# A feed-forward's output product as three products of rounded halves, split by ScalarE and GpSimd

## The chip, the cores and the metric

The kernel runs on one core of a Trainium2 chip. It has five engines: TensorE (PE; its weight loads are shown apart, as PEld), VectorE (DVE), ScalarE (ACT), GpSimd (POOL) and SyncE (SP, here it only issues DMAs). The metric is the device time of one execution in microseconds (us). Lower is better.

## The reference

A decoder of two layers on x [16 sequences, 112 rows, 256 features] with a context of 375 rows. Each part adds to x what it computes from the normalised x. Only the last one is touched:

```python
logits = x @ Wg.T + bg                       # 4 experts, the two best of each row count
w = the softmax weights of the two best, else 0
base = x @ Wi.T                              # 1024 features
lora = (x @ A[e].T) @ B[e].T                 # rank 4, one for each expert e
h = relu(base + lora)                        # [row, expert, 1024]
out = sum_e w[e] * (h[e] @ Wo.T)             # Wo: 256 x 1024
x = x + out
```

All is float32.

## The kernel before

The program is a sequence of phases, each one block in which every engine has its own instruction stream, ordered by hand. Engines wait for each other by semaphores only. The last two phases matter here.

**Last phase (`l1_experts`, tiles named `l1f_`).** The 16 sequences are worked through in G = 4 groups of GB = 4, so a group has GT = 448 rows of x. The 1024 hidden features are FC = 8 chunks f of 128. For the two experts of a row the hidden values are `z_first` and `z_first + change`, and what the output product needs is `h = relu(z_first) + ratio * relu(z_first + change)`, a tile of 128 x 448 for each f.

TensorE, for a group (the body at L2568 to L2585): for each f one product for `change` (L2566), then the products of chunk f + 2 for `z_first`: two wide ones in float32 (L2524, each recorded as two instructions) and one narrow one (L2552). Chunks 0 and 1 of the next group come behind f = 7. Then the output product: for each sequence j of the group eight products, h[f, 112 rows of j] (weights, 112 columns) by wo[f] (moving, 256 columns), summed in one bank of `y_ps` (L2583). In the float32 form each is recorded as two instructions. For j = 0 it waits before each f for the h of that f, since VectorE may still be at work on it. Narrow products, L2552 and L2566, are of kind fp32r already: values that were rounded to fewer bits, for which the engine makes a single pass.

ScalarE copies `z_first` out of its bank (L2495). VectorE makes three instructions for each f: L2451 `z_second = z_first + change_ps` (one input in SBUF, one in PSUM), L2454 `z_second = max(z_second, 0) * ratio_rows` and L2459 `h = max(z_first, 0) + z_second` (both with two inputs in SBUF). Behind f = 7 it takes the four sequences' results out of `y_ps` (L2466), each when TensorE is done with it. GpSimd does nothing in these loops. Groups 1 and 2 run in a loop on the chip (`over_steps`), groups 0 and 3 are written out.

**The phase before (`l1_context_mix`, tiles named `l1x_`).** Its four groups end with a normalisation. VectorE works through, for a group, 4 x (L2165 sum, L2168 and L2170 statistics), 4 x L2174 (`z`, two inputs in SBUF), then waits for `y_rstd`, 4 x L2182 (new x, two inputs in SBUF), 4 x L2186 and L2190 (statistics of x). GpSimd, for a group: L2132 (`y_in` of the next group), 4 x L2149 (x plus a row vector), L2137 and L2139 (`y_rstd` from the statistics), L2125 and L2127 (`rstd` of the group before). SyncE loads the weights of the last phase during it, `l1f_wo` among them.

The same split into rounded halves is used in `l0_cross_attention` (tiles `l0x_`): L987 to L989 and L996 to L998 are three fp32r products each.

## Time and profile before

| | |
|---|---|
| median of 3 runs | 1867.79 us (1864.09 to 1875.49) |
| the profiled execution | 1861.0 us, its span 1859.2 us |
| mean granted TensorE clock | 0.965 of full |
| busy: PE | 1689.0 us, 91% |
| busy: VectorE, ScalarE, GpSimd | 1009.9, 740.9, 658.7 us |
| GpSimd in `l0_cross_attention`, slices 7 to 22 of the span | four to five tenths busy |

The span is that from the first to the last instruction. The last phase fills it from 1690.8 us on, its loops from 1739.6 us. A granted clock of 1.00 is 2.4 GHz, 0.50 is 1.2 GHz. A matmul's recorded duration contains its way through the array; what it costs in a row of matmuls is the distance of their starts. In the rows below "128*112 128x256" reads: weights of 128 rows and 112 columns, moving tile 128 x 256. Every view gives fp32r and float32 tiles as f32 where TensorE reads them.

### The profile page before, as it was taken

How to read it: one execution, taken by the hardware profiler on the slowest of the kernel's cores; microseconds unless marked ns; L12 is line 12 of the kernel's file. 1: busy time of each engine (PE TensorE's matmuls, PEld its weight loads, DVE VectorE, ACT ScalarE, POOL GpSimd, SP SyncE). 2: the span in 40 equal slices, each digit the busy share in tenths (PEclk: the TensorE clock that was granted, in tenths of full speed). 3: DMA queues.
4: the chain of work that ended last, by engine and by line, in shares of the span. 5: the costliest groups of instructions: out<-in, count | busy, mean ns of one | idle time of the engine just before them, and what ended most of it. 6: DMA issues, size and time to landing. Idle time of an engine off the chain costs nothing. (4 is left out here: it accounts for less than half of the span.)

```text
span 1859.2 us, 32555 instructions
## 1 busy us (share of the span) xinstructions
PE 1689.0 (91%) x11198; PEld 1331.6 (72%) x11198; DVE 1009.9 (54%) x2462; ACT 740.9 (40%) x2093; POOL 658.7 (35%) x559
## 2 busy tenths in 40 slices
PE   7899899999999999999999967999889688886898
PEld 6677677777777777777777756899688466554666
DVE  5466465665555665665555532232363577655664
ACT  2255344454444444454444412343113566541210
POOL 1022245555444555554454514343500233352000
PEclk9899999999999999999999979999989799997999
DMA  3100200000000000000000035753300000010000
GB/s 95 54 1 1 98 22 10 10 10 9 9 9 0 9 9 9 9 9 9 9 3 6 1 102 170 246 182 123 103 20 1 1 1 1 1 56 1 0 20 20
DMA packets 48803, 67.39 MB, mean 36 GB/s; under 512 B 11826, under 2 KB 42770, under 8 KB 46034
## 3 DMA queue, kind: packets, MB, share of 16 engines
q1 hardware_dynamic: 47186, 62.66, 10.8%
q0 software_dynamic: 1536, 3.67, 0.6%
q8 instruction: 48, 0.79, 0.2%
q14 instruction: 33, 0.27, 0.0%
HBM read 57.02 MB, written 9.31 MB: 36 GB/s over the span
## 5 line engine op out<-in xcount | busy, mean ns | idle before, releaser
L688 POOL TENSOR_SCALAR l0x_p<-l0x_p,l0x_inv 112x488 f32<-112x488 f32 x256 | 387.2, 1524 | 365.6 <-DVE l0x_inv L782 365.6
L891 ACT ACTIVATE l0x_p<-l0x_s,l0x_low 112x488 f32<-112x488 f32 x256 | 178.4, 697 | 288.0 <-DVE l0x_low L771 288.0
L771 DVE CUSTOM_DVE_ANT_0 l0x_s<-l0x_score_ps,l0x_bias 112x488 f32<-112x488 f32 x256 | 160.3, 664 | 128.5 <-PE l0x_score_ps L1031 117.2
L758 DVE TENSOR_TENSOR l0x_kT_lo<-l0x_proj_ps,l0x_kT_hi 128x488 fp32r<-128x488 f32 x128 | 85.3, 667 | 104.3 <-ACT l0x_kT_hi L881 104.3
L1039 PE MATMUL l0x_pT_ps<-ident,l0x_p 112*122 112x112 f32 x1024 | 124.8, 262 | 13.9 <-POOL l0x_p L688 13.8
L1039 PEld LDWEIGHTS l0x_pT_ps<-ident,l0x_p 112*122 112x122 f32 x1024 | 107.8, 139 | 35.4 <-POOL l0x_p L688 22.8
L1904 POOL TENSOR_TENSOR l1a_pn<-l1a_p,l1a_inv 112x1792 f32<-112x1792 f32 x16 | 50.9, 3184 | 227.7 <-DVE l1a_inv L1932 227.7
L1052 PEld LDWEIGHTS l0x_oT_ps<-l0x_pT,l0x_v 122*64 122x64 f32 x2048 | 100.6, 138 | 43.1 <-issue 32.6
L1052 PE MATMUL l0x_oT_ps<-l0x_pT,l0x_v 122*64 122x112 f32 x2048 | 127.8, 267 | 3.9 <-DVE l0x_pT L777 3.1
L1979 ACT ACTIVATE l1a_p<-l1a_p,l1a_shift 112x112 f32<-112x112 f32 x256 | 95.3, 373 | 63.0 <-DVE l1a_shift L1926 63.0
L987 PE MATMUL l0x_proj_ps<-l0x_kvT_hi,l0x_wkv_hi 128*128 128x488 f32 x256 | 110.4, 431 | 3.0 <-DVE l0x_kvT_lo L746 3.0
L996 PE MATMUL l0x_proj_ps<-l0x_wkv_hi,l0x_kvT_hi 128*122 128x512 f32 x256 | 106.3, 415 | 0.0
L997 PE MATMUL l0x_proj_ps<-l0x_wkv_lo,l0x_kvT_hi 128*122 128x512 f32 x256 | 101.0, 395 | 0.0
L998 PE MATMUL l0x_proj_ps<-l0x_wkv_hi,l0x_kvT_lo 128*122 128x512 f32 x256 | 100.8, 394 | 0.0
L989 PE MATMUL l0x_proj_ps<-l0x_kvT_hi,l0x_wkv_lo 128*128 128x488 f32 x256 | 98.9, 386 | 0.0
L988 PE MATMUL l0x_proj_ps<-l0x_kvT_lo,l0x_wkv_hi 128*128 128x488 f32 x256 | 98.8, 386 | 0.0
L881 ACT ACTIVATE l0x_kT_hi<-l0x_proj_ps 128x488 fp32r<-128x488 f32 x128 | 72.7, 568 | 34.4 <-PE l0x_proj_ps L989 34.4
L777 DVE COPY l0x_pT<-l0x_pT_ps 122x448 f32<-122x448 f32 x128 | 79.1, 618 | 12.8 <-PE l0x_pT_ps L1039 12.8
L2044 PE MATMUL l1a_y_ps<-l1a_wo,l1a_oT 128*112 128x256 f32 x256 | 63.8, 406 | 19.1 <-ACT l1a_oT L1987 19.1
L1663 PE MATMUL l0f_hT_ps<-l0f_xsT,l0f_w 128*128 128x128 f32 x672 | 80.2, 279 | 0.0
L1663 PEld LDWEIGHTS l0f_hT_ps<-l0f_xsT,l0f_w 128*128 128x128 f32 x672 | 78.4, 195 | 0.1
L363 POOL TENSOR_TENSOR l0a_pn<-l0a_p,l0a_inv 112x896 f32<-112x896 f32 x16 | 26.9, 1684 | 139.0 <-DVE l0a_inv L399 139.0
(359 smaller groups left out, 3697.4 us busy)
## 6 DMA issues: line engine op xcount, KB each, us to landing
l0f_w<-in_l0f_w SPq DMA_DIRECT2D x21, 1024.0 KB
l0x_c_in<-in_ctx SPq DMA_DIRECT2D x16, 375.0 KB
l0f_context<-in_ctx SPq DMA_DIRECT2D x16, 375.0 KB
sorted_x<-l0x_zeros SPq DMA_DIRECT2D x1, 2816.0 KB, 14.9
l0f_xs<-sorted_x SPq DMA_DIRECT2D x21, 128.0 KB, 2.2
sorted_y<-l0f_ys SPq DMA_DIRECT2D x21, 128.0 KB, 1.7
l0x_wkv<-in_l0x_wkv SPq DMA_DIRECT2D x2, 1024.0 KB, 9.5
x<-in_x SPq DMA_DIRECT2D x4, 448.0 KB, 8.5
```

Of the source, the lines that this page charges most:

```text
L688: nc.gpsimd.tensor_scalar(p[:, i % 2, a, :], p[:, i % 2, a, :], inv[:, i % 2, a:a + 1], None, ALU.mult).then_inc(pn_ready, 1)
L771: nc.vector.tensor_tensor_reduce(s_sb[:, h % 2, :], score_ps[0:S, h % 2, 0:KEYS], bias[:], -SCALE, 3.4e38, ALU.add, ALU.min, low[:, h:h + ...
L891: nc.scalar.activation(p[:, h // 2 % 2, h % 2, :], s_sb[:, h % 2, :], ACT.Exp, scale=-1.0, bias=low[:, h:h + 1], accum_out=total[:, h:h + ...
L987: nc.tensor.matmul(out, wkv_hi[:, c, at], kvT_hi[:, c, :], start=(c == 0), stop=False)
L988: nc.tensor.matmul(out, wkv_hi[:, c, at], kvT_lo[:, c, :], start=False, stop=False)
L989: done = nc.tensor.matmul(out, wkv_lo[:, c, at], kvT_hi[:, c, :], start=False, stop=(c == KC - 1))
L996: nc.tensor.matmul(out, kvT_hi[:, c, keys], wkv_hi[:, c, at], start=(c == 0), stop=False)
L997: nc.tensor.matmul(out, kvT_hi[:, c, keys], wkv_lo[:, c, at], start=False, stop=False)
L998: done = nc.tensor.matmul(out, kvT_lo[:, c, keys], wkv_hi[:, c, at], start=False, stop=(c == KC - 1))
L1039: done = nc.tensor.transpose(pT_ps[0:KT, a, t * S:(t + 1) * S], p[:, i % 2, a, t * KT:(t + 1) * KT], ident[0:S, 0:S])
L1052: done = nc.tensor.matmul(oT_ps[a * DH:(a + 1) * DH, 0, (i % 4) * S:(i % 4 + 1) * S], v[:, t, (2 * i + a) * DH:(2 * i + a + 1) * DH], pT[: ...
L1663: done = nc.tensor.matmul(hT_ps[:, 2 * (i % 2) + f // 4, (f % 4) * 128:(f % 4 + 1) * 128], w1[:, i % 3, c, f * 128:(f + 1) * 128], xsT[:, ...
```

## The change

1. The product h by wo becomes three fp32r products: h_hi by wo_hi, h_hi by wo_lo, h_lo by wo_hi, where `_hi` is the value rounded to fp32r and `_lo` what is left.
2. h is split for each f: ScalarE copies it to `h_hi`, GpSimd subtracts, `h_lo = h - h_hi` (three inputs and outputs in SBUF). `h` itself becomes a ring of 4 chunks. ScalarE's loop is now: copy of z_first for chunk f + 2, then wait for h of f, then `h_hi` of f.
3. wo is split once, in the phase before: ScalarE makes `wo_hi` in two instructions of 128 x 1024 (in its groups 0 and 1), GpSimd `wo_lo` in eight of 128 x 256 (in its groups 1 and 2, one behind each L2149).
4. The tile x1 of the last phase lies where an earlier phase kept its own, to make room.

```diff
@@ l1_context_mix, gpsimd
+            def split_next(f):
+                pool.wait_ge(next_hi, f // 4 + 1)
+                nc.gpsimd.tensor_tensor(next_w.wo_lo[:, f], next_w.wo[:, f], next_w.wo_hi[:, f].bitcast(F32), ALU.subtract)
                 for b in range(g * GB, (g + 1) * GB):
                     pool.wait_ge(x1_ready, b + 1)
                     nc.gpsimd.tensor_tensor(x[:, b, :], x[:, b, :], rows[:, 2, :], ALU.add).then_inc(ln_b_added, 1)
+                    if g in (1, 2):
+                        split_next(b - GB)
@@ l1_context_mix, scalar, behind take_queries(g + 1)
+                if g < 2:
+                    act.wait_ge(next_w_w, 16 * len(next_w.loads(A)))
+                    nc.scalar.activation(next_w.wo_hi[:, 4 * g:4 * g + 4], next_w.wo[:, 4 * g:4 * g + 4], ACT.Copy
+                                         ).then_inc(next_hi, 1)
@@ l1_experts
-        h = ph.sb("h", [128, FC, GT])
+        h = ph.sb("h", [128, 4, GT])
+        h_hi, h_lo = ph.sb("h_hi", [128, FC, GT], F32R), ph.sb("h_lo", [128, FC, GT], F32R)
@@ l1_experts, gpsimd
+            def body(g, first, last):
+                for f in range(FC):
+                    since(pool, h_hi_ready, g * FC + f + 1)
+                    nc.gpsimd.tensor_tensor(h_lo[:, f, :], h[:, f % 4, :], h_hi[:, f, :].bitcast(F32), ALU.subtract
+                                            ).then_inc(h_lo_ready, 1)
+            over_steps(pool, body, G)
@@ l1_experts, vector
-                    if f == 0:
-                        since(dve, y_done, g * GB)
-                    nc.vector.scalar_tensor_tensor(h[:, f, :], z_first[:, f % 4, :], 0.0, z_second[:, f % 2, :], ALU.max, ALU.add
+                    since(dve, h_lo_ready, n - 3)
+                    nc.vector.scalar_tensor_tensor(h[:, f % 4, :], z_first[:, f % 4, :], 0.0, z_second[:, f % 2, :], ALU.max, ALU.add
                                                    ).then_inc(h_step, 1)
@@ l1_experts, scalar
             def body(g, first, last):
                 for f in range(FC):
-                    n = g * FC + f
-                    since(act, first_done, n + 1)
-                    since(act, h_step, n * 3 - 9)
-                    nc.scalar.activation(z_first[:, f % 4, :], z_ps[:, f % 2, 0:GT], ACT.Copy).then_inc(first_ready, 1)
+                    if f + 2 < FC:
+                        take_first(g, f + 2)
+                    elif not last:
+                        take_first(g + 1, f + 2 - FC)
+                    since(act, h_step, (g * FC + f) * 3 + 3)
+                    if f == 0:
+                        since(act, y_done, g * GB)
+                    nc.scalar.activation(h_hi[:, f, :], h[:, f % 4, :], ACT.Copy).then_inc(h_hi_ready, 1)
@@ l1_experts, tensor
                         if j == 0:
-                            pe.wait_ge(h_step, (g * FC + f) * 3 + 3)
-                        done = nc.tensor.matmul(y_ps[0:S, j % 2, 0:D], h[:, f, j * S:(j + 1) * S], wo[:, f, :],
-                                                start=(f == 0), stop=(f == FC - 1))
+                            pe.wait_ge(h_lo_ready, g * FC + f + 1)
+                        hi, lo = h_hi[:, f, j * S:(j + 1) * S], h_lo[:, f, j * S:(j + 1) * S]
+                        nc.tensor.matmul(y_ps[0:S, j % 2, 0:D], hi, wo_hi[:, f, :], start=(f == 0), stop=False)
+                        nc.tensor.matmul(y_ps[0:S, j % 2, 0:D], hi, wo_lo[:, f, :], start=False, stop=False)
+                        done = nc.tensor.matmul(y_ps[0:S, j % 2, 0:D], lo, wo_hi[:, f, :], start=False, stop=(f == FC - 1))
```

Where the instructions stand. GpSimd in `l1_context_mix`, third group, before:

```order
L2132 TENSOR_TENSOR l1x_y_in<-l1x_x,l1x_rows 112x256 x4
L2149 TENSOR_TENSOR x<-x,l1x_rows 112x256 x4
L2137 TENSOR_SCALAR l1x_y_rstd<-l1x_y_mv 112x4
L2139 TENSOR_TENSOR l1x_y_rstd<-l1x_y_rstd,half 112x4
L2125 TENSOR_SCALAR rstd<-mv 112x4
```

and in the changed kernel, whose line numbers are higher from here on (L2154 is the old L2149, L2142 the old L2137):

```order
L2133 TENSOR_TENSOR l1x_y_in<-l1x_x,l1x_rows 112x256 x4
L2154 TENSOR_TENSOR x<-x,l1x_rows 112x256
L2137 TENSOR_TENSOR l1f_wo_lo<-l1f_wo,l1f_wo_hi 128x256
L2154 TENSOR_TENSOR x<-x,l1x_rows 112x256
L2137 TENSOR_TENSOR l1f_wo_lo<-l1f_wo,l1f_wo_hi 128x256
L2154 TENSOR_TENSOR x<-x,l1x_rows 112x256
L2137 TENSOR_TENSOR l1f_wo_lo<-l1f_wo,l1f_wo_hi 128x256
L2154 TENSOR_TENSOR x<-x,l1x_rows 112x256
L2137 TENSOR_TENSOR l1f_wo_lo<-l1f_wo,l1f_wo_hi 128x256
L2142 TENSOR_SCALAR l1x_y_rstd<-l1x_y_mv 112x4
L2144 TENSOR_TENSOR l1x_y_rstd<-l1x_y_rstd,half 112x4
```

Four subtractions stand between the additions and the two instructions that make `y_rstd`. ScalarE in the last phase's last group, which before was one row of eight copies of z_first and now begins:

```order
L2516 ACTIVATE l1f_z_first<-l1f_z_ps 128x448
L2530 ACTIVATE l1f_h_hi<-l1f_h 128x448
L2516 ACTIVATE l1f_z_first<-l1f_z_ps 128x448
L2530 ACTIVATE l1f_h_hi<-l1f_h 128x448
L2516 ACTIVATE l1f_z_first<-l1f_z_ps 128x448
```

Each copy of z_first is followed by one of h, of the chunk two before.

## Rows read from the trace of the kernel before

**Rows 1.** Chain that ended last, 1660 to 1860 us: start us, length us, instructions.

```profile
1785.23 13.81 PE l1f_y_ps L2583 x64
...
1814.35 13.83 PE l1f_y_ps L2583 x64
...
1843.15 0.64 DVE l1f_h L2459
1843.83 11.06 PE l1f_y_ps L2583 x50
```

**Rows 2.** Groups of instructions, 1738 to 1860 us: busy us, mean ns, idle before.

```profile
L2583 PE MATMUL l1f_y_ps<-l1f_wo,l1f_h 128*112 128x256 f32 x256 | 56.2, 379 | 0.8 <-DVE l1f_h L2459 0.8
...
L2459 DVE SCALAR_TENSOR_TENSOR l1f_h<-l1f_z_first,l1f_z_second 128x448 f32<-128x448 f32 x32 | 20.0, 625 | 1.3
```

**Rows 3.** Timeline at the start of the last group: start us, us, engine, line.

```profile
1827.81 0.56 PE L2566 MATMUL l1f_change_ps<-l1f_low_change,l1f_low_b_r 80*128 80x448 f32 x1
...
1828.74 0.61 DVE L2451 TENSOR_TENSOR l1f_z_second<-l1f_z_first,l1f_change_ps 128x448 f32<-128x448 f32 x1
...
1829.38 0.62 DVE L2454 SCALAR_TENSOR_TENSOR l1f_z_second<-l1f_z_second,l1f_ratio_rows 128x448 f32<-128x448 f32 x1
...
1830.04 0.62 DVE L2459 SCALAR_TENSOR_TENSOR l1f_h<-l1f_z_first,l1f_z_second 128x448 f32<-128x448 f32 x1
```

**Rows 4.** Timeline of PE: fp32r products in `l0x_`, and float32 ones in `l1x_`.

```profile
799.64 0.38 PE L987 MATMUL l0x_proj_ps<-l0x_kvT_hi,l0x_wkv_hi 128*128 128x488 f32 x1
...
800.29 0.39 PE L996 MATMUL l0x_proj_ps<-l0x_wkv_hi,l0x_kvT_hi 128*122 128x512 f32 x1
...
800.99 0.39 PE L996 MATMUL l0x_proj_ps<-l0x_wkv_hi,l0x_kvT_hi 128*122 128x512 f32 x1
...
1654.38 1.95 PE L2263 MATMUL l1x_cT_ps<-l1x_qT,mix 128*128 128x112 f32 x16
```

**Rows 5.** Lines L363 and L2484: duration ns min/median/max.

```profile
L363 POOL TENSOR_TENSOR l0a_pn<-l0a_p,l0a_inv x16: 1682/1684/1687, 81.6 to 204.6; 112x896 f32<-112x896 f32 x16
...
L2484 ACT ACTIVATE l1f_low_first<-l1f_low_masked x4: 576/577/577, 1729.7 to 1737.8; 80x448 fp32r<-80x448 f32 x4
```

**Rows 6.** Timeline of `l1x_`: VectorE's L2182 beside GpSimd.

```profile
1657.19 0.72 POOL L2132 TENSOR_TENSOR l1x_y_in<-l1x_x,l1x_rows 112x256 f32<-112x256 f32 x1
1657.24 0.95 DVE L2182 SCALAR_TENSOR_TENSOR x<-l1x_z,l1x_y_rstd,x 112x256 f32<-112x256 f32 x1
...
1657.87 0.91 POOL L2132 TENSOR_TENSOR l1x_y_in<-l1x_x,l1x_rows 112x256 f32<-112x256 f32 x1
```

**Rows 7.** Line L2182: duration ns min/median/max.

```profile
L2182 DVE SCALAR_TENSOR_TENSOR x<-l1x_z,l1x_y_rstd,x x16: 477/480/949, 1657.2 to 1688.7; 112x256 f32<-112x256 f32 x16
```

**Rows 8.** Line L758, VectorE with one input in PSUM: duration ns min/median/max.

```profile
L758 DVE TENSOR_TENSOR l0x_kT_lo<-l0x_proj_ps,l0x_kT_hi x128: 666/667/669, 225.9 to 1026.9; 128x488 fp32r<-128x488 f32 x128
```

**Rows 9.** Timeline of `l1x_`, third group: GpSimd, then VectorE.

```profile
1669.83 2.96 POOL L2132 TENSOR_TENSOR l1x_y_in<-l1x_x,l1x_rows 112x256 f32<-112x256 f32 x4
1672.74 2.78 POOL L2149 TENSOR_TENSOR x<-x,l1x_rows 112x256 f32<-112x256 f32 x4
1676.38 0.52 POOL L2137 TENSOR_SCALAR l1x_y_rstd<-l1x_y_mv 112x4 f32<-112x4 f32 x1 [0.85 <-DVE l1x_y_mv L2170]
...
1676.32 1.67 DVE L2174 SCALAR_TENSOR_TENSOR l1x_z<-l1x_y,l1x_y_mv,l1x_rows 112x256 f32<-112x256 f32 x4
1678.14 1.67 DVE L2182 SCALAR_TENSOR_TENSOR x<-l1x_z,l1x_y_rstd,x 112x256 f32<-112x256 f32 x4
```

**Rows 10.** Two stretches: us, busy us of each engine, granted clock, DMA.

```profile
1530.00:1540.00 10.00, 8.37 (x72) 6.26 (x70) 7.06 (x9) 6.34 (x31) 3.18 (x1) 1.00 0.01 2
...
1680.00:1690.00 10.00, 2.18 (x8) 1.25 (x8) 9.55 (x31) 0.00 (x0) 5.41 (x8) 0.87 0.00 0
```

**Rows 11.** Timeline of ScalarE and GpSimd behind the first two groups of `l1x_`.

```profile
1654.58 0.92 ACT L2211 ACTIVATE l1x_x1T<-l1x_xT_ps 128x896 f32<-128x896 f32 x1 [3.23 <-PE l1x_xT_ps L2245]
...
1666.71 0.53 POOL L2137 TENSOR_SCALAR l1x_y_rstd<-l1x_y_mv 112x4 f32<-112x4 f32 x1 [3.28 <-DVE l1x_y_mv L2170]
```

More of the change, by code:

```diff
@@ L2111, in l1_context_mix @@
         z_ready, x_step = ph.sem("z_ready"), ph.sem("x_step")
+        next_hi = ph.sem("next_hi")
         block = ctx.enter_context(nc.Block())
@@ L2293, in __init__ @@
         ph = Phase(nc, ctx, "l1f", side="right")
-        self.wi, self.wo = ph.sb("wi", [128, KC, F]), ph.sb("wo", [128, F // 128, D])
+        self.wi = ph.sb("wi", [128, KC, F])
+        self.wo_hi, self.wo_lo = ph.sb("wo_hi", [128, F // 128, D], F32R), ph.sb("wo_lo", [128, F // 128, D], F32R)
         self.wg, self.low_a = ph.sb("wg", [128, KC, E]), ph.sb("low_a", [128, KC, LOW_ROWS])
@@ L2297, in __init__ @@
         self.bg, self.row_expert = ph.sb("bg", [S, E]), ph.sb("row_expert", [S, LOW_ROWS])
+        self.staging = ExitStack()
+        self.wo = Phase(nc, self.staging, "l1f", side="right").sb("wo", [128, F // 128, D])
     def loads(self, A):
@@ L2305, in loads, with l1_experts @@
                 (self.wo[:], A["l1f_wo"].rearrange("(c p) n -> p c n", p=128)))
-def l1_experts(nc, x, stats, norms, w, ident, passed, A, out):
+def l1_experts(nc, x, stats, norms, w, rows_spare, ident, passed, A, out):
     E, R, F = 4, 4, 1024
@@ L2324, in l1_experts @@
     mv, half, rstd, _ = norms
-    wi, wo, wg, low_a, low_b, bg, row_expert = w.wi, w.wo, w.wg, w.low_a, w.low_b, w.bg, w.row_expert
+    wi, wo_hi, wo_lo, wg, low_a, low_b, bg, row_expert = w.wi, w.wo_hi, w.wo_lo, w.wg, w.low_a, w.low_b, w.bg, w.row_expert
     with ExitStack() as ctx:
@@ L2328, in l1_experts @@
         low_b_r = ph.sb("low_b_r", [ER, F], F32R)
-        x1, x1T = ph.sb("x1", [S, B, D]), ph.sb("x1T", [128, KC, B * S])
+        x1, x1T = rows_spare, ph.sb("x1T", [128, KC, B * S])
         logits, best, best_no = ph.sb("logits", [S, B, 8]), ph.sb("best", [S, B, 8]), ph.sb("best_no", [S, B, 8], U32)
@@ L2357, in l1_experts @@
         h_step, y_done, x_step = ph.sem("h_step"), ph.sem("y_done"), ph.sem("x_step")
+        h_hi_ready, h_lo_ready = ph.sem("h_hi_ready"), ph.sem("h_lo_ready")
         GROUP_STEPS = 1 + 2 * GB
@@ L2488, in _, with take_first @@
                                      ).then_inc(ratio_ready, 1)
+            def take_first(g, f):
+                n = g * FC + f
+                since(act, first_done, n + 1)
+                since(act, h_step, n * 3 - 9)
+                nc.scalar.activation(z_first[:, f % 4, :], z_ps[:, f % 2, 0:GT], ACT.Copy).then_inc(first_ready, 1)
+            take_first(0, 0)
+            take_first(0, 1)
             def body(g, first, last):
                 for f in range(FC):
-                    n = g * FC + f
-                    since(act, first_done, n + 1)
-                    since(act, h_step, n * 3 - 9)
-                    nc.scalar.activation(z_first[:, f % 4, :], z_ps[:, f % 2, 0:GT], ACT.Copy).then_inc(first_ready, 1)
+                    if f + 2 < FC:
[6 more added lines that the diff above has]
+                    nc.scalar.activation(h_hi[:, f, :], h[:, f % 4, :], ACT.Copy).then_inc(h_hi_ready, 1)
             over_steps(act, body, G)
@@ L2622, in program @@
             l1_context_mix(nc, x, stats, norms, mix, flag, mix_w, expert_w, ident, passed, A)
-            l1_experts(nc, x, stats, norms, expert_w, ident, passed, A, out)
+            expert_w.staging.close()
+            l1_experts(nc, x, stats, norms, expert_w, router[1], ident, passed, A, out)
 def constants():
```

## The prediction

> **What bounds the kernel now.** I read the page's shares first (TensorE busy 91% of the span), then the chain that ended last, then the groups of the last loops, then timelines. In the loops of the last phase the chain is TensorE's nearly everywhere. A group lasts 1814.35 - 1785.23 = 29.12 us, of which the output product takes 13.8 us and the products of the hidden features the other 15.3 us, 1.9 us for a chunk f [rows 1]. Only in the last group does VectorE end last: its last h ends at 1843.15 + 0.63 = 1843.78, TensorE goes on at 1843.83 with 50 of its 64 output instructions [rows 1], and this is the only wait of the product [rows 2]. The reader is to see how close VectorE runs behind TensorE: seven steps of f, from 1830.04 to 1843.15, take 1.87 us each against TensorE's 1.91 [rows 1, 3]. It has some 2% to spare. Whatever lengthens VectorE's step shows in the time, and whatever shortens TensorE's product does so only as far as VectorE's h arrive.
>
> **The output product.** Before, an instruction of it costs 0.216 us (from 50 in 11.06 us and 64 in 13.82 us, 0.38 of them the last one's own way), so a product of two costs 0.431 us [rows 1]. After, it is three fp32r instructions of 256 columns. The trace has such instructions of 488 columns, (800.29 - 799.64) / 3 = 0.217 us apart, and of 512, 0.233 us apart [rows 4], 0.444 to 0.456 ns a column. In proportion 256 columns cost 0.116 us. If what 512 columns cost above the bare stream (0.213 us at 2.4 GHz) were fixed, it would be 0.127; with nothing above it 0.107. A weight load could forbid this: three loads for 0.348 us instead of two for 0.431. But loads of 128 columns go by every (1.95 - 0.28) / 15 = 0.111 us next to L2263 [rows 4], and these have 112. I take 0.116, so 0.348 us a product, 11.1 us a group instead of 13.8.
>
> The Trainium skill ("TensorE: Matmul & The Clock Gate", Back-to-back issue gap) gives N / 2.4 + 2.5 ns at full clock, 0.109 us for 256 columns. The float32 rows here fit that form, the fp32r rows cost 11 to 17 ns more than it gives; an estimate by the page would make the sum below 2.1 us smaller (300 instructions on the path).
>
> **The split of h.** The h of chunk f now passes ScalarE and GpSimd. ScalarE's copy of the same size takes 0.577 us [rows 5]. GpSimd's subtraction of two SBUF tiles is not there at 448 columns. At 256 it takes 0.72 us [rows 6] and at 896 1.684 us [rows 5], 1.5 ns a column, so 1.01 us. With 0.05 us for each of three handovers (as from 1843.78 to 1843.83 [rows 1]) the half h_lo is ready 0.05 + 0.58 + 0.05 + 1.01 + 0.05 = 1.74 us behind h. ScalarE has two such copies, under 1.2 us, in a step of 1.9 and is no bound, GpSimd neither by itself. ScalarE's order (z_first of f + 2 ahead of h_hi of f) costs nothing while TensorE is ahead. The ring of four makes VectorE wait for a subtraction four steps back, long done.
>
> **What the subtraction does to VectorE.** This is the term that decides. L2182 has two SBUF inputs. Its median is 0.48 us [rows 7], and four take 1.67 us where GpSimd has tiles of four columns [rows 9]. Beside GpSimd's 256-column addition one takes 0.95 us: it starts at 1657.24, GpSimd's ends at 1657.91, it ends at 1658.19, 0.28 us later. The next addition, started at 1657.87, takes 0.91 instead of 0.72 and ends at 1658.78, 0.59 us behind that end [rows 6]. The two exclude each other. A VectorE instruction that reads PSUM is not touched: L758 takes 666 to 669 ns in all of 128 cases [rows 8], in a phase in which GpSimd is busy four to five tenths of the time. So L2451 is free, and L2454 and L2459 exclude the new subtraction.
>
> A step, counted from the end E of h (L2459). L2459 starts 0.66 us behind L2454 [rows 3], so the next L2454 starts 1.87 - 0.66 = 1.21 behind L2459's start, at E + 0.59, and ends at E + 1.21. GpSimd starts at E + 0.68, finds VectorE reading, and ends 0.59 us behind L2454's end, plus 0.29 for the longer tile: E + 2.09. L2459 meanwhile waits and ends 0.28 us later, plus 0.20 for its longer tile (0.15 by durations [rows 2, 7], 0.26 by the distances 0.40 and 0.66 [rows 3, 9]): E + 2.57. A step becomes 2.57 us instead of 1.87, **+0.70 us**, for seven of the eight steps of a group (the first has no subtraction beside it).
>
> **The sum for a group.** Last group, counted from its start at 1827.81 [rows 3]: last h at 15.97 + 7 x 0.705 = 20.9, its h_lo at 22.65. TensorE then has chunk 7 of the first sequence and three whole sequences left, 75 instructions, 8.70 us: 31.35. Before, the last output instruction was over at 1843.83 + 50 x 0.216 = 1854.6, which is 26.8. So +4.5 us. Groups 0 to 2: 31.35 against 29.12, +2.2 each, +6.7. TensorE's own 2.7 us of gain in a group lies in its waits. Loops together: **+11.2 us**.
>
> **The split of wo.** ScalarE's first instruction (1024 columns, under 2.3 times the 0.577 us of 448 [rows 5]) lies in a gap of 3.23 us [rows 11], the second at the same place of the next group: 0. GpSimd's first four take 4 x 0.68 = 2.7 us, in a gap of 3.28 [rows 11]: 0, but with 0.5 us left. In the third group the gap is 0.85 us [rows 9]. There eight instructions start at 1672.74, 0.68 apart; by 1676.32 five are done, and the other three meet VectorE's four L2174, which have two SBUF inputs, at the paired distance of 0.87 us [rows 6]: done at about 1678.9 instead of before 1676.38. What is late next is y_rstd, 1.76 us behind, and L2182, which goes from 1678.14 to 1680.7. VectorE has nothing to make it up with, it is busy 9.55 of the 10 us behind [rows 10]. **+2.5 us** (1.8 if the pairs cost nothing, 3.0 if all four meet).
>
> **The sum.** 1861.0 (the profiled execution) + 11.2 + 2.5 = 1874.7 us. The median of the runs shown lies 6.8 us higher, and on that footing it is 1867.8 + 13.7 = **1881.5 us**, +0.7%.
>
> **Rivals.**
> - *The order in the pair flips.* GpSimd comes only 0.09 us behind L2454. If it gets in first, it ends at E + 1.69, L2454 at 2.17, and L2459, now with its full 0.63 us behind it, at 2.83. 28 steps x 0.26: +7, **1888.6**. For it: the margin is small. Against: both offsets come from rows. 15%.
> - *The subtraction waits whole.* In the rows the delayed addition ends 0.59 us behind VectorE, 0.13 less than its length, as if its first part ran along. If a delayed subtraction needs its full 1.01 us, 28 x 0.13 = +3.6, **1885.1**. Against: the row of 0.91 us. 12%. This is what the Trainium skill has ("SBUF — State Buffer", SBUF: two separate sides): the shared port pair is an exclusive lock that one holds for the whole instruction, against VectorE with two SBUF inputs too. The trace agrees that they exclude each other, and shows the shorter figure.
> - *No exclusion (the other side).* If L2454 and L2459 run on beside the subtraction, as L758 does, h_lo of chunk 7 is there at 15.97 + 1.74 = 17.7, just when TensorE wants it (15.3 + 7 x 0.348). Three groups gain 2.7, the last 0.4, the wo split costs 1.8: -6.6, **1861.2**. It decides from a step below 1.9 us on. Against it stand four L2182 at 0.95. 11%.
> - *The clock falls.* TensorE would idle about a quarter of VectorE's steps. At 1530 to 1540 us it is busy 8.37 of 10 us and its clock stays 1.00 [rows 10]. If it fell to half in these steps, a TensorE step of 3.8 us would exceed 2.57, +10 us a group: **1921**. 6%.
> - *256 columns don't go in one pass.* As float32, a product would cost 3 x 0.431: 25 on the path of each group, +94 us, **1976**. The kind is that of rows 4. 2%.
>
> **How the numbers follow.** The forecast has 50%, its own range 1877 to 1887 (0.107 to 0.127 us an instruction is -2.7 to +3.3 us, the wo term -0.7 to +0.5, the 0.20 above +-1.4). 4% is for what I don't see. The range of 8 in 10 leaves out the last two rivals and most of the one without exclusion: 1864 to 1891. One per cent, 18.7 us, is about what a measurement of this kernel can tell from no change. Slower by more, above 1886.5: the flipped order, a third of the next, the edge of the forecast, clock and passes, together 30%. Faster by more, below 1849.1, no case reaches: 2%. Within: 68%.
>
> **What would show it.** Right: L2454 or L2459 at about 1.3 us instead of 0.63 (the other unchanged), h_lo mostly above 1.0 us, h 2.6 us apart, L2451 still 0.62; output instructions 0.116 us apart, and one TensorE wait of several us before chunk 7 in each group, released by GpSimd; L2182 of the third `l1x_` group 2 to 3 us later. Wrong: L2454 and L2459 both at 0.63 beside the subtraction (then the gain comes through), the fp32r distance above 0.13 us, or a granted clock of 0.5 in the loops.

## The result

| | before | after |
|---|---|---|
| median of 6 runs, timed beside each other | 1871.64 us | 1892.4 us |
| ratio to before, 95% interval | | 1.0089 [1.0046, 1.0132]; timed again 1.0096 [1.0057, 1.0135] |
| span of the profiled execution | 1859.2 us | 1875.9 us |
| mean granted TensorE clock | 0.965 | 0.959 |
| first h to last output instruction ("loops") | 1742.04 to 1854.50, 112.5 us | 1742.01 to 1871.32, 129.3 us |
| from the first normalised row of the `l1x_` phase | 1633.64 to 1854.50, 220.9 us | 1630.95 to 1871.32, 240.4 us |

The change makes the kernel slower by 0.9%, by this ratio some 17 us; forecast were 13.7 us. In the two traces the difference behind the first row of the `l1x_` phase is 19.5 us: 16.8 in the loops, 2.7 in the `l1x_` phase. The execution profiled after happened to come to that phase 2.7 us earlier, so that the whole spans differ by 16.7 us.

In the kernel after, L2474, L2477 and L2481 are the old L2451, L2454 and L2459 (VectorE's three instructions of a step), L2601 the old L2566, L2619 to L2621 the output product, L2401 the new subtraction on GpSimd. The groups of instructions of VectorE and GpSimd in the loops (count, busy us, mean ns, idle before), for [rows 2]:

```profile
L2401 POOL TENSOR_TENSOR l1f_h_lo<-l1f_h,l1f_h_hi 128x448 fp32r<-128x448 f32 x32 | 46.2, 1443 | 121.6 <-ACT l1f_h_hi L2530 121.6
L2481 DVE SCALAR_TENSOR_TENSOR l1f_h<-l1f_z_first,l1f_z_second 128x448 f32<-128x448 f32 x32 | 42.5, 1329 | 1.6
L2477 DVE SCALAR_TENSOR_TENSOR l1f_z_second<-l1f_z_second,l1f_ratio_rows 128x448 f32<-128x448 f32 x31 | 19.4, 625 | 1.3 <-DVE l1f_z_second L2474 0.2
L2474 DVE TENSOR_TENSOR l1f_z_second<-l1f_z_first,l1f_change_ps 128x448 f32<-128x448 f32 x31 | 18.9, 609 | 0.6 <-PE l1f_change_ps L2601 0.4 <-issue 0.2
```

h takes 1.33 us instead of 0.625, the other two as before. The end of the second group, timelines of VectorE and GpSimd, shows why:

```profile
1789.89 1.44 DVE L2481 SCALAR_TENSOR_TENSOR l1f_h<-l1f_z_first,l1f_z_second 128x448 f32<-128x448 f32 x1
1791.26 0.61 DVE L2474 TENSOR_TENSOR l1f_z_second<-l1f_z_first,l1f_change_ps 128x448 f32<-128x448 f32 x1
1791.90 0.63 DVE L2477 SCALAR_TENSOR_TENSOR l1f_z_second<-l1f_z_second,l1f_ratio_rows 128x448 f32<-128x448 f32 x1
1792.56 1.47 DVE L2481 SCALAR_TENSOR_TENSOR l1f_h<-l1f_z_first,l1f_z_second 128x448 f32<-128x448 f32 x1
...
1792.02 1.52 POOL L2401 TENSOR_TENSOR l1f_h_lo<-l1f_h,l1f_h_hi 128x448 fp32r<-128x448 f32 x1 [1.17 <-ACT l1f_h_hi L2530]
1794.71 1.13 POOL L2401 TENSOR_TENSOR l1f_h_lo<-l1f_h,l1f_h_hi 128x448 fp32r<-128x448 f32 x1 [1.18 <-ACT l1f_h_hi L2530]
```

GpSimd starts at 1792.02, 0.12 us behind L2477, and ends at 1793.54, 1.01 us behind L2477's end at 1792.53. L2481 starts at 1792.56 and ends 0.49 us behind the subtraction (0.99 and 0.48 us in the steps ahead of this one). The last subtraction of a group has nobody beside it and takes 1.13 us. The step is 1792.56 - 1789.89 = 2.67 us.

TensorE: the start of its first `change` product in groups 1, 2 and 3; its waits in the last phase (us in total, times, longest us); and the output product of its last group:

```profile
1772.61 0.37 PE L2601 MATMUL l1f_change_ps<-l1f_low_change,l1f_low_b_r 80*128 x1
...
1804.73 0.37 PE L2601 MATMUL l1f_change_ps<-l1f_low_change,l1f_low_b_r 80*128 x1
...
1837.42 0.37 PE L2601 MATMUL l1f_change_ps<-l1f_low_change,l1f_low_b_r 80*128 80x448 f32 x1
```

```profile
PE l1f_change_ps L2601 <- DVE l1f_z_second L2474: 8.6, 5, 2.2
PE l1f_y_ps L2619 <- POOL l1f_h_lo L2401: 7.6, 6, 2.0
```

```profile
1860.60 0.55 PE L2619 MATMUL l1f_y_ps<-l1f_wo_hi,l1f_h_hi 128*112 128x256 f32 x1 [1.31 <-POOL l1f_h_lo L2401]
1860.95 0.41 PE L2620 MATMUL l1f_y_ps<-l1f_wo_lo,l1f_h_hi 128*112 128x256 f32 x1
1861.16 0.41 PE L2621 MATMUL l1f_y_ps<-l1f_wo_hi,l1f_h_lo 128*112 128x256 f32 x1
...
1864.94 0.28 PE L2621 MATMUL l1f_y_ps<-l1f_wo_hi,l1f_h_lo 128*112 128x256 f32 x1
1865.06 0.28 PE L2619 MATMUL l1f_y_ps<-l1f_wo_hi,l1f_h_hi 128*112 128x256 f32 x1
...
1871.32 0.28 PE L2621 MATMUL l1f_y_ps<-l1f_wo_hi,l1f_h_lo 128*112 128x256 f32 x1
```

The first three groups take 32.5, 32.1 and 32.7 us (29.4, 29.1 and 29.1 before), the last one 1871.32 - 1837.42 = 33.9 (26.7 before, [rows 1, 3]). The output instructions are 0.12 us apart at full clock and 0.21 us up to 1864.8, where the clock stood at half after TensorE's waits. Before, the granted clock was 1.00 through all the loops. Now it is 0.95 over each of the first three groups and 0.85 over the last: behind TensorE's waits in the last steps of a group it falls for a short stretch (windows: length, busy us of PE, PEld, DVE, ACT and POOL, granted clock, DMA):

```profile
1787.00:1790.50 3.50, 3.50 (x7) 1.93 (x7) 3.40 (x5) 0.67 (x3) 2.33 (x2) 0.61 0.00 0
...
1857.00:1865.00 8.00, 5.39 (x24) 5.07 (x25) 2.18 (x3) 0.58 (x1) 2.37 (x2) 0.57 0.01 2
```

The wo split in the third `l1x_` group, GpSimd and then VectorE (L2181 and L2189 are the old L2174 and L2182), for [rows 9]:

```profile
1673.27 0.71 POOL L2137 TENSOR_TENSOR l1f_wo_lo<-l1f_wo,l1f_wo_hi 128x256 fp32r<-128x256 f32 x1
1673.95 0.90 POOL L2154 TENSOR_TENSOR x<-x,l1x_rows 112x256 f32<-112x256 f32 x1
1674.82 0.91 POOL L2137 TENSOR_TENSOR l1f_wo_lo<-l1f_wo,l1f_wo_hi 128x256 fp32r<-128x256 f32 x1
1675.69 0.40 POOL L2142 TENSOR_SCALAR l1x_y_rstd<-l1x_y_mv 112x4 f32<-112x4 f32 x1
...
1673.42 2.97 DVE L2181 SCALAR_TENSOR_TENSOR l1x_z<-l1x_y,l1x_y_mv,l1x_rows 112x256 f32<-112x256 f32 x4
1677.33 1.67 DVE L2189 SCALAR_TENSOR_TENSOR x<-l1x_z,l1x_y_rstd,x 112x256 f32<-112x256 f32 x4 [0.93 <-POOL l1x_y_rstd L2144]
```

Four L2181 take 2.97 us (1.67 before), and the first L2189 comes 3.91 us behind the first L2181 (1.82 before). That is 2.1 us. Another 0.8 us is lost behind it, through TensorE's clock. TensorE now waits 4.49 us for VectorE instead of 2.41, and the same eight products take 3.40 us instead of 2.18, at a granted clock of 0.63 (1681 to 1685 us) where it was 1.00 before; VectorE waits for them. Before, then after:

```profile
1681.83 2.18 PE L2273 MATMUL l1x_o_ps<-l1x_wo,l1x_cT 128*112 128x256 f32 x8 [2.41 <-DVE l1x_y L2165]
...
1681.02 3.40 PE L2284 MATMUL l1x_o_ps<-l1x_wo,l1x_cT 128*112 128x256 f32 x8 [4.49 <-DVE l1x_y L2172]
```

### The profile page after: what moved, and what is told of

Read it like the earlier page. It is cut to its first block and busy times, and to the rows that moved or that the text cites. A ratio compares the mean times of both kernels' runs of the same rounds, so it can differ in the third digit from the quotient of the medians.

```text
span 1875.9 us, 32938 instructions
## 1 busy us (share of the span) xinstructions
PE 1687.7 (90%) x11326; PEld 1337.3 (71%) x11326; DVE 1032.4 (55%) x2462; ACT 759.0 (40%) x2127; POOL 710.2 (38%) x599
## 5 line engine op out<-in xcount | busy, mean ns | idle before, releaser
L758 DVE TENSOR_TENSOR l0x_kT_lo<-l0x_proj_ps,l0x_kT_hi 128x488 fp32r<-128x488 f32 x128 | 85.3, 666 | 104.5 <-ACT l0x_kT_hi L881 104.5
L1039 PE MATMUL l0x_pT_ps<-ident,l0x_p 112*122 112x112 f32 x1024 | 124.8, 262 | 13.7 <-POOL l0x_p L688 13.7
L2401 POOL TENSOR_TENSOR l1f_h_lo<-l1f_h,l1f_h_hi 128x448 fp32r<-128x448 f32 x32 | 46.2, 1443 | 121.6 <-ACT l1f_h_hi L2530 121.6
L363 POOL TENSOR_TENSOR l0a_pn<-l0a_p,l0a_inv 112x896 f32<-112x896 f32 x16 | 26.9, 1683 | 139.1 <-DVE l0a_inv L399 139.1
```

Source lines behind the costliest of these rows:

```text
L1039: done = nc.tensor.transpose(pT_ps[0:KT, a, t * S:(t + 1) * S], p[:, i % 2, a, t * KT:(t + 1) * KT], ident[0:S, 0:S])
```

## The experiments

The theory: VectorE's h (two SBUF inputs) and GpSimd's subtraction shut each other out, this alone lengthens VectorE's step, and VectorE becomes the bound of the loops. Rivals: the new products and their weight loads; ScalarE's copy and the longer way to h_lo; the clock; the wo split. In the table "step" is the distance of two h in us once it is steady (without a disturbance it varies from 1.85 to 1.94 and a mean stands there), "h" and "subtraction" are the mean length of one such instruction in ns, "group" is the second one, "last" the last one up to the start of the last output instruction, "loops" runs from the first h to there; all three in us. The expectations of the first four versions that were run (no subtraction, subtraction on VectorE, one input, split alone) count the loops from 1739.6 us to the end of VectorE's last instruction, 3.3 us more than the table's (115.8 us before). Ratios are to the kernel before, timed beside each on the same chip; the chips differ. Two versions were executed once and have no ratio: only their traces are used. In the code below `...` stands for lines left out.

| kernel | ratio, interval | step | h | subtraction | group | last | loops |
|---|---|---|---|---|---|---|---|
| before | 1 | 1.87 | 625 | | 29.1 | 26.7 | 112.5 |
| after | 1.0089 [1.0046, 1.0132] | 2.67 | 1329 | 1443 | 32.1 | 33.9 | 129.3 |
| after, second trace | 1.0096 [1.0057, 1.0135] | 2.67 | 1328 | 1443 | 32.1 | 33.9 | 129.1 |
| no subtraction | 0.9962 [0.9927, 0.9997] | 1.88 | 625 | | 26.6 | 26.8 | 105.1 |
| subtraction on VectorE | 1.0029 [0.9996, 1.0061] | 2.39 | 625 | 619 | 29.3 | 30.3 | 116.7 |
| one input on GpSimd | | 2.08 | 820 | 1636 | 28.2 | 29.6 | 113.2 |
| split alone | 1.0118 [1.0057, 1.0179] | 2.67 | 1338 | 1442 | 33.3 | 33.9 | 131.6 |
| GpSimd behind the last h | | 1.86 | 625 | 1136 | 33.8 | 33.8 | 134.1 |
| two halves | 1.0047 [1.0018, 1.0077] | 2.19 | 913 | 981 | 28.9 | 30.6 | 116.2 |
| four quarters | 1.0092 [1.0053, 1.0132] | 1.95 | 706 | 592 | 31.6 | 31.6 | 126.3 |
| filler | 1.0103 [1.0063, 1.0142] | 2.67 | 1184 | 1388 | 34.3 | 33.6 | 134.5 |
| less filler | 1.0118 [1.0083, 1.0152] | 2.67 | 1234 | 1406 | 33.0 | 32.3 | 129.2 |
| wo split late | 1.0086 [1.0046, 1.0127] | 2.67 | 1302 | 1434 | 32.1 | 33.6 | 133.7 |
| subtraction later, on VectorE | 0.9964 [0.9931, 0.9997] | 1.86 | 625 | 2022 | 26.7 | 27.3 | 108.8 |

### Without the subtraction

```diff
-                    nc.gpsimd.tensor_tensor(h_lo[:, f, :], h[:, f % 4, :], h_hi[:, f, :].bitcast(F32), ALU.subtract
-                                            ).then_inc(h_lo_ready, 1)
...
-                    since(dve, h_lo_ready, n - 3)
+                    since(dve, h_hi_ready, n - 3)
...
-                            pe.wait_ge(h_lo_ready, g * FC + f + 1)
-                        hi, lo = h_hi[:, f, j * S:(j + 1) * S], h_lo[:, f, j * S:(j + 1) * S]
+                            pe.wait_ge(h_hi_ready, g * FC + f + 1)
+                        hi, lo = h_hi[:, f, j * S:(j + 1) * S], h_hi[:, f, j * S:(j + 1) * S]
```

> The changed kernel without GpSimd's subtraction of h: TensorE reads h_hi in place of h_lo (same number, shape and kind of instructions, so the result leaves out the low part of h). ScalarE's copy h_hi stays. Theory (VectorE's two-input instructions and GpSimd's subtraction exclude each other, and this sets the step): VectorE's step falls from 2.67 back to 1.87 us, h at 0.63 us, a group takes 15.3 + 11.1 = 26.4 us instead of 32.1 (before the change 29.1), the last one 15.97 + 0.68 + 8.7 = 25.3, the loops 106 us instead of 132 (before 116), granted clock 1.00 in them; with the 2 us of the wo split the time is about 7 us below the kernel before. Rival A (the fp32r products and their three weight loads, or ScalarE's extra copy, slow the step): the step stays above 2.4 us and the loops above 125 us. Rival B (the longer way h, h_hi, h_lo alone): the step was never long for it, only 1 us a group comes back, loops about 128 us.

Two windows of it (length, busy us of PE, PEld, DVE, ACT and POOL, granted clock, DMA):

```profile
1755.00:1785.00 30.00, 30.00 (x156) 22.44 (x155) 19.37 (x34) 9.84 (x20) 0.00 (x0) 1.00 0.05 16
1785.00:1815.00 30.00, 30.00 (x156) 22.36 (x155) 19.13 (x34) 10.60 (x20) 0.00 (x0) 1.00 0.06 16
```

In these windows TensorE is busy throughout at full clock, and the group takes 26.6 us for 26.4 expected. The same three products, loads and ScalarE copies are in it, so neither they nor the way over ScalarE are the cause. Of the 24.2 us by which its loops are shorter than those after, the first three groups have 5.4 to 6.1 each and the last 7.1. The last group took 26.8 us, not 25.3: the clock was at half for part of it (0.94 over the group). The version leaves out h_lo, so its ratio of 0.9962 is no gain that can be had; it shows where the time goes.

### The split alone, in the kernel before

```diff
...
+                    since(act, h_step, (g * FC + f) * 3 + 3)
+                    since(act, h_lo_ready, g * FC + f - 1)
+                    nc.scalar.activation(h_hi[:, f % 2, :], h[:, f, :], ACT.Copy).then_inc(h_hi_ready, 1)
...
+                    since(pool, h_hi_ready, g * FC + f + 1)
+                    since(pool, h_lo_ready, g * FC + f)
+                    nc.gpsimd.tensor_tensor(h_lo[:, 0, :], h[:, f, :], h_hi[:, f % 2, :].bitcast(F32), ALU.subtract
+                                            ).then_inc(h_lo_ready, 1)
```

> The kernel before with only the split of h added (ScalarE's copy and GpSimd's subtraction into small rings that nobody reads); the float32 output product and wo are untouched. Theory: the subtraction alone makes the step 2.6 to 2.7 us; the last h comes at 21.4 of a group instead of 15.97, and 25 float32 products of 0.431 follow: group 32.2 us instead of 29.1, last 32.2 instead of 26.8, loops 130 us against 116, time 13 to 15 us above the kernel before. Rival (the new product and its clock are the cause): loops within 2 us of 116.

Timeline of VectorE in the second group; L2470 is h:

```profile
1782.32 0.62 DVE L2464 SCALAR_TENSOR_TENSOR l1f_z_second<-l1f_z_second,l1f_ratio_rows 128x448 f32<-128x448 f32 x1
1782.98 1.44 DVE L2470 SCALAR_TENSOR_TENSOR l1f_h<-l1f_z_first,l1f_z_second 128x448 f32<-128x448 f32 x1
1784.35 0.61 DVE L2461 TENSOR_TENSOR l1f_z_second<-l1f_z_first,l1f_change_ps 128x448 f32<-128x448 f32 x1
1784.99 0.62 DVE L2464 SCALAR_TENSOR_TENSOR l1f_z_second<-l1f_z_second,l1f_ratio_rows 128x448 f32<-128x448 f32 x1
1785.64 1.44 DVE L2470 SCALAR_TENSOR_TENSOR l1f_h<-l1f_z_first,l1f_z_second 128x448 f32<-128x448 f32 x1
```

A subtraction whose result nobody reads, together with ScalarE's copy, makes the same step, 2.66 us, and 19 us in the loops, with the old product and the old wo. With the run above, in which the copy stays and the step is back at 1.88 us, this shows the cause from both sides. The loops are 5 us longer than I expected. The first group, at full clock, took 32.4 us for 32.2 expected. The others took 33.3 to 33.9 us, with the clock at 0.95 (0.90 in the last): TensorE waits up to 2.2 us in them, and the products behind such a wait run at half clock.

### The subtraction alone and undisturbed

GpSimd makes the same 32 subtractions, but all eight of a group behind the last h_hi; all eight h are kept for it. TensorE does the products with h_hi of two sequences first, and wo is split late (below).

```diff
-                    since(pool, h_hi_ready, g * FC + f + 1)
+                    since(pool, h_hi_ready, g * FC + FC)
```

> As the version with the subtraction after the last h, but GpSimd makes it, in the same 32 instructions of 448 columns as in the changed kernel, while VectorE has nothing but results to write. It measures the disputed instruction alone. If the 1.44 us that it takes in the changed kernel are waiting for VectorE: 1.0 to 1.13 us each (the last of a group takes 1.13 in the changed kernel), 8.2 to 9 us for eight; if it is slow by itself: 1.4 to 1.5 us. VectorE's step is 1.87 us, h at 0.63 us in both cases. The group is then 16.6 + 8.2 to 9 for the eight h_lo, + 6.7 us for what TensorE has left, 31.5 to 32.3 us, as long as in the changed kernel, with the same GpSimd instructions and a step of 1.87 instead of 2.67.

```profile
L2404 POOL TENSOR_TENSOR l1f_h_lo<-l1f_h,l1f_h_hi 128x448 fp32r<-128x448 f32 x32 | 35.2, 1136 | 129.5 <-ACT l1f_h_hi L2534 129.5
```

1.14 us each: of the 1.44 in the kernel after 0.3 come from VectorE beside it, and my estimate of 1.01 was 0.13 short. h is back at 0.625 us. The group is 33.8 us, 1.5 over the expectation; TensorE waits for eight subtractions in a row, and behind that it runs in part at half clock (0.90 over a group).

### The subtraction on VectorE

```diff
+            def subtract(g, f):
+                dve.wait_ge(h_hi_ready, g * FC + f + 1)
+                nc.vector.tensor_tensor(h_lo[:, f, :], h[:, f % 4, :], h_hi[:, f, :].bitcast(F32), ALU.subtract
+                                        ).then_inc(h_lo_ready, 1)
...
+                    if f >= 1:
+                        subtract(g, f - 1)
+                subtract(g, FC - 1)
```

> The changed kernel with the same 32 subtractions made by VectorE, one step behind h; GpSimd does nothing in the loops. Theory: the step is the sum of four VectorE instructions, 1.87 + 0.62 = 2.49 us, steady; the last h at 15.97 + 7 x 0.62 = 20.3 of a group, h_lo 0.63 + 0.62 behind it, 21.6, group 30.3 us (32.1 with GpSimd), loops 123 us against 132, so that the subtraction costs VectorE less when VectorE does it than when GpSimd does; time about 9 us below the changed kernel and 8 above the one before. Rival (exclusion costs less than an instruction, the step of 2.67 has another cause): the step becomes 2.67 + 0.62 or stays near 2.67 and the loops are not shorter than 132 us.

A fourth instruction costs VectorE about 0.54 us a step (it overlaps a little with its neighbours), and six of the seven intervals of a group have one. GpSimd's cost it 0.80. Loops 116.7 us, as the expectation counts them 120.0 for 123, and 12.6 under the kernel after: the engine that is nearly the bound does the work itself for less than the "idle" engine takes from it. The rival, a step of 2.67 us or more, is out. Against the kernel before nothing is gained; the interval of the ratio holds 1.

### One SBUF input on GpSimd

```diff
-                    nc.gpsimd.tensor_tensor(h_lo[:, f, :], h[:, f % 4, :], h_hi[:, f, :].bitcast(F32), ALU.subtract
+                    nc.gpsimd.tensor_scalar(h_lo[:, f, :], h[:, f % 4, :], 2.0 ** -13, None, ALU.mult
                                             ).then_inc(h_lo_ready, 1)
-            over_steps(pool, body, G)
+            for g in range(G):
+                body(g, g == 0, g == G - 1)
```

> The changed kernel with GpSimd's instruction of two SBUF inputs (h minus h_hi) replaced by one of a single SBUF input, h times a constant, of the same 448 columns, at the same place and behind the same wait (the result leaves out the right low part of h). If the exclusion needs two inputs on GpSimd's side as well: L2477 and L2481 at 0.62 us, step 1.87 us, loops about 108 us. If any GpSimd instruction on SBUF shuts VectorE's two-input instructions out: the step is 1.87 + about 0.5 to 0.8 us, h 1.1 to 1.4 us, loops 123 to 132 us. If GpSimd's instruction is merely shorter (under 0.6 us), the step shrinks by as much as it is shorter.

```profile
1790.90 0.62 DVE L2478 SCALAR_TENSOR_TENSOR l1f_z_second<-l1f_z_second,l1f_ratio_rows 128x448 f32<-128x448 f32 x1
1791.56 0.86 DVE L2482 SCALAR_TENSOR_TENSOR l1f_h<-l1f_z_first,l1f_z_second 128x448 f32<-128x448 f32 x1
...
1791.03 1.69 POOL L2401 TENSOR_SCALAR l1f_h_lo<-l1f_h 128x448 fp32r<-128x448 f32 x1 [0.40 <-ACT l1f_h_hi L2531]
...
1795.19 1.33 POOL L2401 TENSOR_SCALAR l1f_h_lo<-l1f_h 128x448 fp32r<-128x448 f32 x1 [0.40 <-ACT l1f_h_hi L2531]
```

None of the three cases: the instruction is longer by itself (1.33 us against 1.13), yet VectorE loses only 0.2 us a step. h, started at 1791.56, ends at 1792.42, before GpSimd's instruction does at 1792.72. Here the two run along together in part. So between kinds of instruction the longer one need not cost VectorE more. Whether the number of inputs or the kind of operation makes the difference is open: the edit changes both.

### Two halves, four quarters

```diff
+                    for part in (slice(0, GT // 2), slice(GT // 2, GT)):
+                        done = nc.gpsimd.tensor_tensor(h_lo[:, f, part], h[:, f % 4, part], h_hi[:, f, part].bitcast(F32), ALU.subtract)
+                    done.then_inc(h_lo_ready, 1)
```

> The changed kernel with GpSimd's subtraction in two instructions of 224 columns instead of one of 448. If an instruction of GpSimd with two SBUF inputs shuts VectorE out until it ends (in the trace after, h ends 0.49 us behind the subtraction's end), VectorE's h gets in between the halves: it waits for half as long, 0.4 us less, the step is 2.3 to 2.4 us instead of 2.67, a group 30 to 31 us instead of 32.1, loops about 124 us instead of 129.3. If VectorE is shut out by GpSimd's work as such, however it is cut: the step stays at 2.67 us or grows by the second instruction's own 0.1 us.

> GpSimd's subtraction in four instructions of 112 columns (one of 448 in the changed kernel: step 2.67 us; two of 224: 2.19 us). Two views of what the halves gained. If cutting only removes the waiting of VectorE for an instruction's end, four parts halve what is left of it again: excess over 1.87 from 0.80 to 0.32 to about 0.15, step 2.0 us, loops 112 us. If the two engines' access to SBUF adds up, the floor is reached: VectorE's two instructions of 0.63 and GpSimd's about 1.0 us without its fixed part (1.14 for 448 columns and 0.64 for 224 give 0.14 fixed, 1.0 for the columns) make 2.2 to 2.3 us, and GpSimd itself needs 4 x 0.39 = 1.56 us; the step stays at 2.2 to 2.4 us, loops 116 to 121 us.

(The diff is that of the halves.) VectorE and GpSimd with halves, then TensorE's waits and GpSimd with quarters:

```profile
1789.07 0.97 DVE L2482 SCALAR_TENSOR_TENSOR l1f_h<-l1f_z_first,l1f_z_second 128x448 f32<-128x448 f32 x1
...
1791.26 0.97 DVE L2482 SCALAR_TENSOR_TENSOR l1f_h<-l1f_z_first,l1f_z_second 128x448 f32<-128x448 f32 x1
```

```profile
1788.54 2.02 POOL L2402 TENSOR_TENSOR l1f_h_lo<-l1f_h,l1f_h_hi 128x224 fp32r<-128x224 f32 x2 [0.16 <-ACT l1f_h_hi L2531]
1790.73 2.03 POOL L2402 TENSOR_TENSOR l1f_h_lo<-l1f_h,l1f_h_hi 128x224 fp32r<-128x224 f32 x2 [0.17 <-ACT l1f_h_hi L2531]
```

```profile
PE l1f_y_ps L2620 <- POOL l1f_h_lo L2402: 12.7, 14, 2.1
```

```profile
1776.47 13.67 POOL L2402 TENSOR_TENSOR l1f_h_lo<-l1f_h,l1f_h_hi 128x112 fp32r<-128x112 f32 x22
```

VectorE gets in between the pieces: 0.80 us of excess a step, 0.32 with halves, 0.08 with quarters. h takes 1.44, 0.97 and 0.73 us where a piece, with nobody beside it, takes 1.13, 0.66 and 0.41 us: each time 0.31 to 0.32 more than one piece. So VectorE is shut out for the length of one piece, as the theory has it. My view of a floor at 2.2 us is refuted for VectorE. But GpSimd now waits at each piece: 22 quarters in 13.67 us are 2.49 us a chunk, and GpSimd takes VectorE's place as the bound (its last h_lo comes at 21.3 us of a group, VectorE's last h at 16.4). Halves are the better cut here: loops 13 us shorter than after, still 3.8 longer than before, all of it in the last group (30.6 us for 26.7), and the ratio of 1.0047 lies above 1 with its whole interval. Quarters lose most of it again.

### The clock

Products that nobody reads keep TensorE at work while it waits. The second version has smaller ones, and none ahead of the last chunk; the diff is cut from it.

```diff
+                    fill(f, 3 if last and f >= 6 else 1)
                     multiply_change(g, f)
...
+                            if f == 6:
+                                fill(f, 2)
```

> The changed kernel with products that nobody reads added to TensorE where it waits for VectorE and GpSimd: one pair of 160 columns (0.54 us) per step f, four pairs in the last two steps of the last group, three pairs ahead of chunks 6 and 7 of the output product. It tells what the clock costs. Theory: VectorE and GpSimd set the time of the first three groups, the halved clock costs only where it outlasts TensorE's wait: the granted clock stays 1.00 (or falls more rarely), the step stays 2.67, groups stay at 32.1 to 32.5 us, and the last group falls from 34.0 to about 32.2; loops 127 us against 129.3. Rival (the clock is a main cause of the 17 us): groups of 30 us or less, loops below 122 us.

> The filler again, smaller where it held up the product: one pair of 144 columns (0.49 us) per step, three in the last two steps of the last group, two ahead of chunk 6 and none ahead of chunk 7. Theory: granted clock 1.00 in the loops or nearly; step 2.67 us; groups 32.1 to 32.7 us as in the changed kernel; only the last one falls, from 34.0 to 32.2 to 32.5; loops from the first h 127 to 128 us against 129.3, so that the clock's part in the longer loops is about 2 us. Rival (the clock is a main cause): loops below 122 us.

A window of the second version, then two of its h:

```profile
1761.00:1865.00 104.00, 100.43 (x575) 79.51 (x573) 70.62 (x91) 28.33 (x52) 35.22 (x26) 1.00 0.05 14
```

```profile
1802.02 1.45 DVE L2481 SCALAR_TENSOR_TENSOR l1f_h<-l1f_z_first,l1f_z_second 128x448 f32<-128x448 f32 x1
...
1804.69 1.43 DVE L2481 SCALAR_TENSOR_TENSOR l1f_h<-l1f_z_first,l1f_z_second 128x448 f32<-128x448 f32 x1
```

The first filler held up the output product itself (groups of 34.3 us, TensorE busy without a gap), so its times say nothing. The second gives what was asked: with the clock at 1.00 the step is 2.67 us all the same, and only the last group is shorter, by 1.6 us. The filler takes as much in the other groups (33.0 for 32.1 us in the second), so the loops come to 129.2 us and not the 127 to 128 expected. The clock is not the cause of the longer step; in the last group it adds 1.6 us or somewhat more.

### The wo split late

GpSimd subtracts wo_hi in the last phase, behind the normalised x, instead of in the `l1x_` phase.

```diff
-                    if g in (1, 2):
-                        split_next(b - GB)
...
+            pool.wait_ge(x1_ready, B)
+            for f in range(FC):
+                nc.gpsimd.tensor_tensor(wo_lo[:, f], w.wo[:, f], wo_hi[:, f].bitcast(F32), ALU.subtract
+                                        ).then_inc(wo_lo_ready, 1)
```

> The changed kernel with only the subtraction for wo_lo moved: out of the third and fourth eight additions of GpSimd in the l1x phase, to the start of the last phase (over wo's own memory). Theory: in the third l1x group the distance from VectorE's first z (L2181) to its first update of x (L2189) returns from 3.91 to about 1.8 us; the loops are as in the changed kernel (129 us from the first h); time 1 to 2 us below the changed kernel, so a ratio of 1.007 to 1.009 to the kernel before. Rival (the wo split is what costs): a ratio below 1.003.

The distance from VectorE's first z to its first update of x is back at 1.81 us. From the first row of `l1x_` to VectorE's third normalisation of the last phase, the five traces with no wo split in `l1x_` have 57.9 to 58.1 us (before, split alone, GpSimd behind the last h, subtraction later on VectorE, this one), the kernel after 60.7 and 60.8 in its two traces: the split costs 2.7 to 2.9 us there. It doesn't show in the time: the ratio, 1.0086, is that of the kernel after, above the rival's 1.003 with its whole interval, and an interval some 15 us wide cannot show a gain of 2 or 3. In this execution 2.3 us are lost between that normalisation and the first h (52.6 us for 50.3) and 3.5 in the first group, 36.0 us instead of 32.5, whose first products ran near half clock (0.55 from 1745.4 to 1752 us). The move does not cause the first of these: the split alone, where wo is not split at all, has 52.8 us there, and GpSimd behind the last h, which moves the split too, 50.3. For the first group it stays open.

### The subtraction later, on VectorE

What the runs point to: eight h in float32, subtracted in place by VectorE, for a group, in two instructions of 1792 columns while TensorE does the products of h_hi for two sequences; the wo split late.

```diff
+                dve.wait_ge(h_hi_ready, g * FC + FC)
+                for k in range(2):
+                    pair = slice(2 * k * S, 2 * (k + 1) * S)
+                    nc.vector.tensor_tensor(h_lo[:, :, pair], h[:, :, pair], h_hi[:, :, pair].bitcast(F32),
+                                            ALU.subtract).then_inc(h_lo_ready, 1)
```

> A version that keeps the three rounded products but takes the subtraction out of VectorE's steps: all eight h of a group are kept in float32, and VectorE, idle while TensorE does the output product, subtracts in two instructions (sequences 0 and 1, then 2 and 3) after the last h_hi, into the same memory. TensorE first does the products of h_hi for sequences 0 and 1, then those of h_lo. wo_lo is computed by GpSimd at the start of the last phase, where it is idle, over the memory of wo. Theory: step 1.87 us, group 15.3 + 11.3 = 26.6 us (29.1 before the change, 32.1 after), the last about 27, loops from the first h 105 to 106 us (112.5 before, 129.3 after), time 7 to 9 us below the kernel before, ratio 0.995 to 0.996. If a big subtraction comes too late for TensorE (the pair of 1792 columns costs 2.4 us behind h_hi, TensorE has 3.8 us of other work, but started ahead of it), up to 2 us a group are lost, 112 us, ratio 1.000. If the products themselves or their weight loads were the cause of the longer loops, they stay above 125 us.

VectorE from 1770 us on, that is behind the first group's steps:

```profile
L2478 DVE SCALAR_TENSOR_TENSOR l1f_h<-l1f_z_first,l1f_z_second 128x448 f32<-128x448 f32 x24 | 15.0, 625 | 1.0
...
L2483 DVE TENSOR_TENSOR l1f_h_lo<-l1f_h,l1f_h_hi 128x1792 fp32r<-128x1792 f32 x7 | 13.9, 2022 | 2.2 <-ACT l1f_h_hi L2532 2.2
```

A group takes 26.7 us, as without any subtraction: the products' gain of 2.4 us a group is real once VectorE's step is left alone. The time is 0.36% below the kernel before, [0.9931, 0.9997], the only version with the whole computation whose interval lies below 1, and by little. Loops are 108.8 us for 105 to 106: the first group took 29.8 us, at half clock for a part (0.63 from 1747 to 1755 us).

## Why the prediction came out as it did

- **What bounds the loops, and which term decides**: right, and the runs without the subtraction and with it alone show it. The step of VectorE is what moved, by the exclusion of h and the subtraction; L2474, with a PSUM input, is untouched (0.61 us).
- **Size of the step**: forecast 2.57, measured 2.67. Two terms of the working. The subtraction's own length, 1.01 us by columns, is 1.14. The 1.5 ns a column came from the tile of 896 columns [rows 5], a product with a second input that holds one value for each head and row (`inv`), not a second tile of that size; 112, 224 and 448 columns of the subtraction itself (0.41, 0.66, 1.13 us) give 2.1 ns, and this leads from the 0.72 us at 256 [rows 6] to 1.13. And it ends 1.01 us behind L2477, not 0.59 + 0.29 = 0.88. That h ends 0.48 us behind the subtraction was right (0.49). This is nearly the rival "the subtraction waits whole" (step 2.70, 1885.1 us), though by another sum: its full length of 1.01 us was a guess that the longer instruction happens to meet, and 0.13 of its 1.14 us run along. The Trainium skill ("SBUF — State Buffer", SBUF: two separate sides) has a lock for the whole instruction. For two inputs on each side the traces agree to within those 0.13 us; with one input on GpSimd's side they don't: there h ended 0.3 us ahead of GpSimd's instruction. "GpSimd first" did not happen: its start fell 0.12 us behind L2477's in the steady steps.
- **The group**: forecast 31.35 us, measured 32.1 to 32.7. The last h_lo came at 23.1 to 23.7 us instead of 22.65. The rest is the product itself, 0.118 us an instruction instead of 0.116, 8.9 for 8.70 us. TensorE's wait ahead of chunk 7 was to be one of several us; the trace has it in pieces of at most 2.2 us, 8.6 us in all for z_second and 7.6 for h_lo.
- **The clock**: the rival's price was wrong in both ways. It did fall, which had 6%, but in short stretches at the ends of the steps, where VectorE sets the pace; not for a whole group. What it costs is about 2 us in the last group, the first 20 of whose last 75 instructions ran 0.21 us apart until 1864.8 (an estimate: 20 x 0.095 us; the filler gave back 1.6), and 0.8 us in `l1x_`. I had judged by a window with 84% of busy time and full clock [rows 10]; the waits here reach 2.2 us in one piece.
- **Loops**: forecast +11.2, measured +16.8. Three groups +3.0 to +3.6 instead of +2.2, the last +7.2 instead of +4.5.
- **The wo split**: forecast +2.5, measured +2.7 by the phase, in part by luck: 2.1 us are the delay that I had worked out as 2.5, the rest is TensorE's clock behind it, which the sum did not have. Of GpSimd's eight instructions the last two met VectorE's (0.90 and 0.91 us), where I had three; y_rstd is what is late next, as described.
- **The fp32r product**: right, 0.118 us, one pass, with 112-column weight loads hidden.
- **The sum**: +13.7 us forecast against +17 and +18 by the ratios, inside their intervals (+8.6 to +25). Behind the first row of `l1x_` the traces say +19.5 and +19.3: the way is right, the loops were put a third too low. 1892.4 us lies 1.4 above the range of 1864 to 1891; the ratio on the footing of 1867.8 us gives 1884.4.
